# Channel attention as an engine loop, the second batch's transfers ahead of the fourth batch's loads, and constant products in the workspace FFN's first step

## The reference, cut to what matters

```python
x = x + _L0_xattn_ref(_layernorm(x), ctx, ctx)   # channel attention, 8 heads of 16 channels
x = x + _L0_ffn_ref(_layernorm(x), w_up, w_down) # ternary weights, Hadamard transforms
x = x + _L1_xattn_ref(_layernorm(x), ctx, ctx)   # causal attention, 16 heads
x = x + _L1_ffn_ref(_layernorm(x), ...)          # workspace FFN, two rounds
```

```python
qk = jnp.einsum('bdm,bdn->bmn', qh, kh) * scale
sm = jax.nn.softmax(qk, axis=-1)
ret = jnp.einsum('bmn,bcn->bcm', sm, vh)
```

## Time and profile before

| what | value |
|---|---|
| median of 3 runs | 3771.95 us (3765.82 to 3773.39) |
| the profiled execution's own time | 3779.81 us |
| its span | 3777.9 us |
| PE busy | 3537.5 us, 94% |
| DVE busy | 2887.7 us, 76% |
| ACT busy | 2554.2 us, 68% |
| POOL busy | 1741.6 us, 46% |
| channel attention | about 0 to 1600 us |
| ternary FFN | about 1600 to 2240 us |
| causal attention | about 2240 to 2904 us |
| workspace FFN | about 2904 to 3778 us |

### The profile page before, as it was taken

How to read it: one execution, slowest core, us unless ns; L and a number is a source line. 1 busy time by engine, 2 the same in 40 slices (tenths; PEclk the granted TensorE clock), 3 DMA queues, 4 the chain that set the end, 5 groups by cost and what they waited for, 6 DMA issues and landing times. The chain is left out here.

```text
span 3777.9 us, 73028 instructions
## 1 busy us (share of the span) xinstructions
PE 3537.5 (94%) x25219; PEld 1778.8 (47%) x25219; DVE 2887.7 (76%) x4445; ACT 2554.2 (68%) x6417; POOL 1741.6 (46%) x2148
## 2 busy tenths in 40 slices
PE   6999999999999999889999979999997999999997
PEld 1222222222222222278788855555554666666664
DVE  7888888888888888768878858888886466574745
ACT  3777777777777777667777758878875454545454
POOL 5444444444444444077666624554553233342524
PEclk9999999999999999989999989999999999999999
DMA  7777677676677777433333313333452022120402
GB/s 123 123 124 124 120 122 123 118 123 121 120 124 124 124 124 138 125 99 124 116 118 115 117 61 101 108 107 103 129 177 86 1 68 68 41 95 4 132 1 79
DMA packets 344317, 392.11 MB, mean 104 GB/s; under 512 B 58640, under 2 KB 223120, under 8 KB 343952
## 3 DMA queue, kind: packets, MB, share of 16 engines
q1 hardware_dynamic: 316464, 352.03, 42.0%
q10 hardware_dynamic: 27488, 35.41, 3.7%
HBM read 200.65 MB, written 84.93 MB: 76 GB/s over the span
## 5 line engine op out<-in xcount | busy, mean ns | idle before, releaser
L385 DVE TENSOR_REDUCE a_neg_max<-a_max_ps 128x2 f32<-128x1024 f32 x1024 | 1209.9, 1220 | 199.6 <-PE a_max_ps L497 189.9
L529 ACT ACTIVATE a_P<-a_ring_ps 128x512 f32<-128x512 f32 x2048 | 1085.4, 603 | 407.7 <-PE a_ring_ps L477 398.5
L497 PE MATMUL a_max_ps<-a_K,a_Q 96*128 96x512 bf16 x2048 | 621.3, 385 | 32.6 <-DMA a_Q<-a_q_split 24.6
L477 PE MATMUL a_ring_ps<-a_Q,a_K 98*128 98x512 bf16 x2048 | 627.6, 384 | 14.4 <-DMA a_Q<-a_max_rows 10.1
L514 PE MATMUL a_pv_ps<-a_P,a_V 128*32 128x512 f32 x4096 | 545.7, 605 | 1.8 <-ACT a_out_sb L534 1.8
L477 PEld LDWEIGHTS a_ring_ps<-a_Q,a_K 98*128 98x128 bf16 x2048 | 157.9, 96 | 681.4 <-ACT a_P L529 497.8
L1334 ACT ACTIVATE c_P<-c_s_ps,c_bias 128x128 f32<-128x128 f32 x1024 | 368.1, 384 | 65.1 <-DVE c_bias L1170 64.8
L324 POOL TENSOR_SCALAR a_var_eps<-a_mean_var 128x1 f32<-128x1 f32 x64 | 12.3, 192 | 765.1 <-DVE a_mean_var L401 765.1
L497 PEld LDWEIGHTS a_max_ps<-a_K,a_Q 96*128 96x128 bf16 x2048 | 188.9, 98 | 220.8 <-DMA a_Q<-a_q_split 24.6
L1165 DVE TENSOR_REDUCE c_neg_max<-c_s_ps 128x4 f32<-128x512 f32 x256 | 175.7, 686 | 81.5 <-PE c_s_ps L1260 75.0
L1334 ACT ACTIVATION_READ_ACCUMULATOR c_P<-c_s_ps,c_bias 128x1 f32 x1024 | 228.4, 223 | 0.0
(11 more groups left out here) (271 smaller groups left out, 7267.7 us busy)
## 6 DMA issues: line engine op xcount, KB each, us to landing
a_K<-a_k_split SPq DMA_DIRECT2D x384, 128.0 KB, 7.1
a_Q<-a_q_split SPq DMA_DIRECT2D x378, 128.0 KB, 4.6
heads_out<-a_out_sb ACTq DMA_DIRECT2D x128, 256.0 KB, 4.6
w_first_in<-in_x_dram SPq DMA_DIRECT2D x112, 256.0 KB, 3.6
w_second_in<-in_ctx_dram SPq DMA_DIRECT2D x64, 256.0 KB, 4.9
w_third_in<-in_ctxT_dram SPq DMA_DIRECT2D x64, 256.0 KB, 5.0
x<-b_x SPq DMA_DIRECT2D x64, 256.0 KB, 2.1
c_x_in<-x SPq DMA_DIRECT2D x64, 256.0 KB, 3.6
```

Of the source, the lines that this page charges most:

```text
L385: dve.tensor_reduce(neg_max[:, p, 2 * u:2 * u + 2], max_ps[u % 2][:, :, :], AX.X, ALU.max, negate=True).then_inc(max_taken, 1)
L477: pe.matmul(ring(s, use_of(k))[:, :], K[i][:, h, n:n + 128], Q[i][:, h, :], start=True, stop=True).then_inc(scores_filled, 1)
L497: last = pe.matmul(max_ps[u % 2][:, j, :], Q[i][0:KROW, h, m:m + 128], K[i][0:KROW, h, :], start=True, stop=True)
L529: act.activation(P[p][k // NT][:, k % NT, :], ring(s, use_of(k))[:, :], ACT.Exp, scale=SCALE).then_inc(exp_done, 1)
```

## The change

Three parts:

1. `run_steps` becomes a loop on each engine: the first and last steps stay written out, and those between `loop_from` and `loop_to` run as 19 (SyncE, GpSimd, VectorE) or 20 (TensorE, ScalarE) turns of six steps. Inside the loop the counts of the waits depend on a register, and the DRAM addresses of loads and stores as well; `Held` adds a semaphore increment behind such a wait. The other stages stay written out.
2. SyncE issues the transfers of batch 1 (step k=-2) ahead of the loads of batch 3; in all other steps the order is as before. GpSimd copies v of batch 0 at k=-5, behind the k split of batch 0, instead of at k=-3 behind the presets.
3. In the workspace FFN's first step TensorE executes 36 extra products (2, 11, 2, 5, 14 and 2 at six places) of a constant 128x128 bf16 tile by 512 columns of the same tile, into a PSUM bank that nobody reads at that time. VectorE sets the tile once, at the start of the causal attention. `w_raw` is gone; its two uses work in place on `e_top`.

```diff
-def run_steps(eng, first, last, body):
+def run_steps(eng, first, loop_from, loop_to, last, body):
-    for k in range(first, last + 1):
+    assert (loop_to - loop_from) % 6 == 0
+    for k in range(first, loop_from):
         body(Step(0, k))
+    with eng.Fori(0, (loop_to - loop_from) // 6) as turn:
+        for k in range(6):
+            body(Step(turn, loop_from + k))
+    for k in range(loop_to, last + 1):
+        body(Step(0, k))
+def keep_busy(pe, bank, tile, n):
+    for _ in range(n):
+        pe.matmul(bank, tile[:, :], tile[:, :].unsqueeze(1).to_broadcast([128, 4, 128]), start=True, stop=True)
...
+                if s.k == -2:
+                    transfer_parts(s)
+                load_rows(s)
...
+                if s.k != -2:
+                    transfer_parts(s)
+            run_steps(sp, -8, 2, 116, 126, step)
...
+                if s.half(3) == 0 and s.exists(3) and s.k != -3:
+                    split_values(s.batch(3), s.slot(3), s.lap(3))
+                if s.k == -5:
+                    split_values(0, 0, 0)
+            run_steps(pool, -6, 4, 118, 126, step)
...
+            run_steps(dve, -7, 1, 115, 125, step)
+            run_steps(pe, -2, 2, 122, 128, step)
+            run_steps(act, -1, 4, 124, 129, step)
...
+            dve.memset(w.spare[:, :], 1.0).then_inc(w.spare_ready, 1)
...
                     last.then_inc(l_filled, 1)
+                    if f.k == 0:
+                        keep_busy(pe, xb_ps[1][:, :], w.spare, 2)
...
(behind L1872: 11; behind L1882: 2; ahead of L1900: 5; ahead of L1922: 14; ahead of L1823: 2)
```

More of the change, by code:

```diff
@@ L247, in load_weights, with load_rows, transfer_parts @@
                 sp.dma_start(w_in[:, c, :].rearrange("p (k n) -> p k n", k=src.shape[1]), src).then_inc(w_loaded[c], 16)
+            def load_rows(s):
+                if s.half(8) == 0 and s.exists(8):
+                    b, i = s.batch(8), s.slot(8)
+                    at_least(held, q_split_done, b - (NB - 1))
+                    at_least(held, k_split_done, b - (NB - 1))
+                    at_least(held, v_done, b - (NB - 1))
+                    sp.dma_start(x_in[i][:, :], by_channel(x[b])).then_inc(x_loaded[i], 16)
+                    sp.dma_start(c_in[i][:, :], by_channel(ctx[b])).then_inc(c_loaded[i], 16)
+                    sp.dma_start(cT_in[i][:, :].rearrange("p (t c) -> p t c", t=NT), ctxT[b].rearrange("(t p) c -> p t c", p=128)).then_inc(cT_loaded[i], 16)
+            def transfer_parts(s):
+                if s.half(4) == 0 and s.exists(4):
+                    b, i = s.batch(4), s.slot(4)
+                    if s.k != -4:
+                        held.wait_ge(q_split_done, b + 1)
+                    held.wait_ge(k_split_done, b + 1)
+                    at_least(held, scores_filled, (b - (NB - 1)) * (2 * SCORES))
+                    if s.k != -4:
+                        for n, part in enumerate((0, 0, 1, 1, 0, 2)):
+                            sp.dma_start(Q[i][n * D:(n + 1) * D, :, :], q_split[:, i, part, :]).then_inc(Q_loaded[i], 16)
+                    for n, part in enumerate((0, 1, 0, 1, 2, 0)):
+                        sp.dma_start(K[i][n * D:(n + 1) * D, :, :], k_split[:, i, part, :]).then_inc(K_loaded[i], 16)
             def step(s):
@@ L1424, in workspace_ffn @@
         top, neg_top = sb("top", [128, 8]), sb("neg_top", [128, 1])
-        is_top, e_top, w_raw, w_top = sb("is_top", [128, 128]), sb("e_top", [128, 128]), sb("w_raw", [128, 128]), sb("w_top", [128, 128])
+        is_top, e_top, w_top = sb("is_top", [128, 128]), sb("e_top", [128, 128]), sb("w_top", [128, 128])
         w_sum, w_inv = sb("w_sum", [128, 1]), sb("w_inv", [128, 1])
@@ L1717, in step @@
                     dve.wait_ge(e_top_done, n + 1)
-                    dve.scalar_tensor_tensor(w_raw[:, :], e_top[:, :], 1.0, is_top[:, :], ALU.mult, ALU.mult, accum_out=w_sum[:, :]).then_inc(top_chain, 1)
+                    dve.scalar_tensor_tensor(e_top[:, :], e_top[:, :], 1.0, is_top[:, :], ALU.mult, ALU.mult, accum_out=w_sum[:, :]).then_inc(top_chain, 1)
                     dve.wait_ge(top_chain, n * LINKS + 6)
@@ L1721, in step @@
                     dve.wait_ge(w_top_done, n * 2 + 1)
-                    dve.tensor_scalar(w_top[:, :], w_raw[:, :], w_inv[:, :], None, ALU.mult).then_inc(w_top_done, 1)
+                    dve.tensor_scalar(w_top[:, :], e_top[:, :], w_inv[:, :], None, ALU.mult).then_inc(w_top_done, 1)
                 if u.exists():
```

28 lines of the change are left out of this document (17 added, 11 removed).

## The result

The changed kernel takes 3742.67 us (median of 4 runs, 3736.68 to 3747.78) against 3769.44 (4 runs): the ratio is 0.9928 [0.9909, 0.9947], 27 us less. In a second series on another chip it was 3741.74 against 3764.87, ratio 0.9931 [0.9917, 0.9946], 23 us less. The forecast was 3758.

What follows compares the result with a forecast made beforehand. TensorE was taken to bound the channel attention (97.8% busy), every second group starting when rows DMAs land. Terms -9 (start), -3 (constant products) and -2 (loop) made -14 us, from the median 3771.95 to 3758; range 3745 to 3800.

Steps and rivals of the forecast that it cites:

- Part 1, the loop: Channel attention's six-step turns: -6 us for fetches, +4 for later rows DMAs, together -2 us.
- the lateness: Channel attention: 13 us that 120 groups take beyond 120 quiet ones, taken as partly caused by TensorE's instruction fetches.
- the quiet group: Channel attention: a group not delayed by late rows DMAs, 11.89 us, expected to stay so.
- The fetches: Channel attention loop: TensorE's 62 fetched pieces of 16 KB become fewer, removing half of the fetch lateness, -6 us.
- Register work: Channel attention loop: register operations for the waits hidden in TensorE's free time, but rows DMAs later, +4 us.
- rival C: Channel attention: register work makes rows DMAs half a microsecond later in every second group, +30 us, 3784; chance 0.13.
- Rival A: Channel attention: loop code stays with TensorE and rows DMAs come in time everywhere, total -24 us, 3748; chance 0.20.
- Rival B: Channel attention: each turn's end stalls VectorE or ScalarE for a code fetch, 2.5 us, +48 us, 3806; chance 0.13.
- Part 2, the start: Start of channel attention: earlier batch 1 transfers remove TensorE's stalls of 4.69 and 3.80 us, -9 us.
- the 2 us to be given back in group 1: Start: without the stall TensorE's clock stays higher, so group 1 regains 2 of the 2.4 us above 11.89.
- Part 3, the constant products: Workspace FFN's first step: extra products fill waits and keep TensorE's clock full, -3 us.
- its better case: Workspace FFN's first step: the clock stays full, -4 us; if it falls all the same, +5.5 us.

Runs made afterwards that it cites:

- dve_straight: The changed kernel with VectorE's steps written out while the other four engines loop: 3733.41 us, ratio 0.9916 to the kernel before.
- pe_loop_act_swap: The kernel before with only TensorE looped, ScalarE's two waits swapped, the new transfer order and the constant products: 3731.97 us, ratio 0.9907.
- number 4: Experiment on the looped kernel's late groups: the changed kernel with K transfers waiting for eight score products, 3742.28 us; also dve_straight. Its timeline shows a late group.
- start_only: The kernel before with only batch 1's transfers ahead of batch 3's loads and the early v copy: 3762.75 us, ratio 0.9996.

## Why the prediction was wrong

The direction was right, but the change gave -27 us (-23 in the second series) where -14 was forecast, and 3742.67 us is 2 us below the range.

- **Part 1, the loop: forecast -2, measured -17.** This is the step that failed. I priced the loop by the lateness alone ("From below: if TensorE's fetches cease, the lateness of 13 us goes, -13") and held the quiet group fixed ("quiet groups still at 11.89"). The quiet group is where the gain came from, 0.14 us each by the form of the waits. A row that I had left aside said it: TensorE stood idle 0.19 us ahead of each L486, for ScalarE, 22.4 us in 120 groups. I reasoned that 130 array instructions need 4.3 us and 7.6 are free. But TensorE and ScalarE take turns, and each hand-over is on the path whatever room the array has; I read 97.8% busy as a bound by the array, where it was in part a chain of hand-overs between overlapping products.
- **The fetches (-6 for half of the lateness).** Right in cause: of before's 13 us of lateness 7.9 stand at the group's first product (10 where the waits are swapped), in 20 groups and not in every second one, and they are gone (0 to 0.7 us) in the changed kernel, dve_straight and pe_loop_act_swap. Wrong in net: they stand in the -17 not at all, because VectorE's register work took as much (9.9 us).
- **Register work (+4, by later rows DMAs; rival C +30).** Right in that register work costs, wrong in the place. The rows DMAs are issued at the same point of the group (4.1 us into it before, 4.0 now). VectorE has 1.6 us free per group as a mean. But in every second group the layer norm's sums stand ahead of four reductions that follow without a break, and what idle time there is (0.41 and 0.48 us in the group of number 4) lies behind these. The mean over a whole group hid it.
- **Rival A (3748)** came nearest in time, by another mechanism: it wanted rows DMAs in time everywhere, and got that, but lost it again at L521.
- **Rival B** does not hold at six steps: 3 + 6 pieces, no idle time at a turn's end. At twelve it costs 9.6 us a jump, and TensorE's own branch (3.5 us), which the rival left out, is more of it than VectorE's stall (2.7 to 3.1 us).
- **Part 2, the start: forecast -9 from one execution (bounds -4.7 to -10.9).** Issue at 23.59 (23.5 forecast), L521 of batch 1 at 44.88 (45.3), step 1 at 55.41 (55.9 to 59.3) all came as worked out or a little better. Of the 2 us to be given back in group 1 there came 14.33 - 12.88 = 1.5. Against the profiled execution of before group 4 starts 10.2 us earlier. But the old start varies: step 1 began at 56.5 to 65.7 us in ten profiles with it (mean 61.2) and at 54.5 to 56.9 in eight with the new one (mean 55.7). Group 4 starts 5.7 us earlier in the mean, and start_only's total gained 1.5 us (interval -5.6 to +2.3). Reading a landing under load off one execution made the term 3 us too large.
- **Part 3, the constant products: forecast -3.** The chain behind them runs at full clock, as in its better case. From the first product to L1834 the step took 42.9 us in ten profiles without them and 40.1 in eight with them, as means: -2.8. Behind the 32 transposes, from L1855 (now L1882) on, it took 33.3 us in all eight and 35.6 to 36.9 in the ten. The transposes themselves took 6.0 to 7.5 us with and without, and 1.0 of the 4.5 us of the two profiled executions stands there by chance. The rest of the difference to the mean is that in other executions without them fewer products were at half clock.

By these the sum is -17 - 6 - 3 = -26, and -23 and -27 were measured.

## What to carry to other kernels

Where two engines hand work to each other many times a group, look at which of two waits ahead of an instruction is the late one and let the instruction itself carry it (here: write it first, and see in the trace which line has the EVENT_SEMAPHORE); that was worth 0.14 us of 11.9 here, more than the fetches. Put a loop only on the engine whose fetches hurt, count register work against the room of its fullest step and not of its mean one, and keep the body short enough to stay: six steps did, twelve cost ten microseconds at each jump. And take a stall at the start from several executions, where it hangs on DMAs under load.

## What the runs showed of the hardware

A second wait ahead of an instruction is an instruction of its own: 51 ns on TensorE, 17 on ScalarE, 21 on VectorE. Register operations in the loop took 32 to 51 ns on TensorE by the medians of their lines, 35 to 42 on ScalarE and 40 to 64 on VectorE. The loop's own at each turn on TensorE, the branch last:

```profile
L94 PEldq FUSED_REGOPS  x20: 68/68/68, 66.7 to 1418.8; - x20
...
L94 PEldq ALU_OP  x20: 32/32/32, 138.0 to 1491.0; - x20
L94 PEldq COMPARE_BRANCH  x20: 76/208/243, 138.1 to 1491.1; - x20
```

The page "Advanced Engine Details and Errata" of the Trainium skill (Control Flow Timing) gives about 108 ns for a compare-and-branch. The traces don't agree with it: by the medians the branch takes 208 ns on TensorE and 45 to 56 on the four other engines. Jumps back to a body of 780 array instructions cost no time that the trace shows on TensorE's path, and to bodies of 1560 and more some 10 us each: 3.3 to 5.3 us in TensorE's branch, 2.7 to 3.1 us behind VectorE's, and a stretch at a lower granted clock.
